# A graph network's first stage: products, turn and counts reordered within each quarter, and the next group's first turn moved into this group's last quarter

## The chip, the core and the metric

The kernel runs on one core of a Trainium2 chip. A core has five engines with a queue of instructions each: PE (TensorE, matrix products), DVE (VectorE), ACT (ScalarE), POOL (GpSimd, which here issues gathers) and SP (SyncE, which issues the other DMAs). They meet only at semaphores: an instruction waits until a counter has reached a value, and another raises it when it is done. The metric is the device time of one launch in microseconds (us); less is better.

## What is computed

The inputs are 12,500 nodes with 32 features, 200,000 edges sorted by target (`dst`) and 16 attributes for each edge. The reference, cut to what matters:

```python
h = relu(layernorm(x))
m = relu(concat([h[src], edge_attr]) @ w1a + b1a) @ w1b + b1b       # one message per edge
agg = segment_sum(m, dst) / max(count(dst), 1)
x = x + relu(concat([h, agg]) @ w2a + b2a) @ w2b + b2b

f = feat0 = relu(layernorm(x))
for _ in range(10):                                                 # propagation
    f = 0.9 * segment_sum((f * out_deg**-0.5)[src], dst) * in_deg**-0.5 + 0.1 * feat0
x = x + f
```

## The kernel before

The program prepares keys and degrees (up to about 185 us), then runs `messages_and_counts` (to about 2825 us), then `nodes_of_runs` (the node layer) and `propagate` (ten steps of dense products with a table of edge counts, from about 3000 us to the end). The change is in `messages_and_counts` alone.

That function does two jobs at once for 98 *groups*. A group g is 16 edges on each of the 128 partitions (2048 edges), and also 32 windows of 4 target nodes. A group has four *quarters* q.

- **Messages.** POOL gathers the source rows of 16 columns of edges, one indirect DMA for each column, into one of seven row buffers, seven groups ahead. PE *turns* a quarter of them (`turn_rows(q)`: two transposes, L1333, into bank `T_BANK`), ACT copies that to SBUF (`keep_turned`, L1262, tile `turn`), PE multiplies it by the weights (`mix(q)`: four float32 products that the profile counts as 8 matmuls, L1351, into `M_BANK`), and ACT applies relu into `run_sums` (`relu_messages`, L1266). DVE adds these along runs of one target (`add_run`, L1184, sixteen in the first half of the next group) and SP stores them.
- **Counts.** DVE makes 0/1 matrices: `part_hot` for a quarter (L1219) and `place_hot` for each of its 8 windows (L1223). PE multiplies them: `count(r)`, r = 0 to 15, four for each quarter, each with two matmuls of L1316 into one of four banks and two of L1322 into a bank of running sums. ACT copies each bank of two counts out (`read_counts(u)`, u = 0 to 7, L1257). I call these copies **read 0 to read 7**; read u needs counts 2u and 2u+1. SP stores them.

On **PE** the order in a group is: turn 0, mix 0, then the sixteen counts, with turn q+1 behind the second count of quarter q and mix q+1 behind its third. `mix(q)` waits until ACT has copied turn q and has applied relu to the products of the quarter before. On odd groups `mix(3)` also turns the keys of the next pair of groups (L1291); on even groups mix 0 waits until DVE has read them (`local_made`). **ACT** follows in the order: copy of turn 0, relu 0, read 0, copy of turn 1, read 1, relu 1, read 2, and so on.

**POOL** (`step`) refills the row buffer of group g in eight pairs of gathers, u = 0 to 7. The first pair waits for turn 3 of group g and for the indices. The others wait for ACT (`count_read`, L1092): pairs 1 and 2 for reads 6 and 7 of group g, and pairs 3 to 7 for reads 0 to 4 of group g+1. On odd groups one gather of keys (L1075) comes before. The last 7 groups have no gathers.

The semaphore `turned` counts the turns; SP (L1133) and POOL (L1082) wait for it by number. PE's and ACT's code runs in a hardware loop of 7 rounds of 14 groups, as DVE's does; POOL's and SP's run 6 rounds and write out the last one.

## Time and profile before

| | |
|---|---|
| median of 3 runs | 7052.78 us (7047.1 to 7060.38) |
| the profiled execution's own time | 7054.22 us |
| its span, first to last instruction | 7052.7 us |
| PE busy in the span | 5638.9 us (80%) |
| DVE busy | 4287.4 us (61%) |
| POOL busy | 1693.6 us (24%) |
| ACT busy | 713.1 us (10%) |

A time of the profiled execution can be compared with the median of the runs directly: they are 1.4 us apart. A share of the whole span is an average over stages that have different limits, so the stage of the change has to be read by itself: it holds nearly all of ACT's and POOL's work and little of PE's. Idle time before an instruction is given with what ended it; "remote" there means that a semaphore rose at a moment at which the records show no instruction ending, and "issue" that nothing it waited for rose just then. A matmul's record starts when the engine takes it; its end is modelled.

### The profile page before, as it was taken

How to read it: one execution, taken by the hardware profiler on the slowest of the kernel's cores; microseconds unless marked ns; L12 is line 12 of the kernel's file. 1: busy time of each engine (PE TensorE's matmuls, PEld its weight loads, DVE VectorE, ACT ScalarE, POOL GpSimd, SP SyncE). 2: the span in 40 equal slices, each digit the busy share in tenths (PEclk: the TensorE clock that was granted, in tenths of full speed). 3: DMA queues.
4: the chain of work that ended last, by engine and by line, in shares of the span. 5: the costliest groups of instructions: out<-in, count | busy, mean ns of one | idle time of the engine just before them, and what ended most of it. 6: DMA issues, size and time to landing. Idle time of an engine off the chain costs nothing. (4 is left out here: it accounts for less than half of the span.)

```text
span 7052.7 us, 211605 instructions
## 1 busy us (share of the span) xinstructions
PE 5638.9 (80%) x85008; PEld 3706.2 (53%) x85008; DVE 4287.4 (61%) x12668; ACT 713.1 (10%) x1695; POOL 1693.6 (24%) x1739
## 2 busy tenths in 40 slices
PE   1455565655555557589999999999999999999998
PEld 1355454544454446446565565656555565656564
DVE  7455555555555557766656666666656666666665
ACT  0122222222222223000000000000000000000000
POOL 5555555555555552500000000000000000000000
PEclk9766666666667667799999999999999999999999
DMA  4322222222222222145555555555555555555554
GB/s 118 76 75 76 75 75 75 75 71 78 73 79 72 75 75 90 37 186 192 200 190 200 190 200 200 190 200 190 200 191 199 191 202 202 187 203 191 199 197 170
DMA packets 442865, 1016.62 MB, mean 144 GB/s; under 512 B 253162, under 2 KB 371914, under 8 KB 387354
## 3 DMA queue, kind: packets, MB, share of 16 engines
q1 hardware_dynamic: 386938, 968.76, 38.8%
q0 software_dynamic: 54944, 33.96, 2.6%
q8 instruction: 714, 11.70, 0.6%
q14 instruction: 269, 2.20, 0.1%
HBM read 838.78 MB, written 176.58 MB: 144 GB/s over the span
## 5 line engine op out<-in xcount | busy, mean ns | idle before, releaser
L1866 PE MATMUL banks_fast<-count_units_fast,feature_parts_fast 128*32 128x512 fp8e3 x70608 | 3826.2, 379 | 31.6 <-DVE count_units_fast L1761 27.0
L1866 PEld LDWEIGHTS banks_fast<-count_units_fast,feature_parts_fast 128*32 128x32 bf16 x70608 | 2154.4, 97 | 1680.2 <-issue 37.4
L1760 DVE TENSOR_SCALAR count_units_fast<-packed_ring_fast 128x512 int32<-128x512 int32 x2949 | 1257.0, 426 | 1427.4 <-PE banks_fast L1866 1396.9
L144 POOL DMA_INDIRECT rows_fast<-row_table,idx_fast x1456 | 1408.6, 967 | 1034.7 <-ACT count_stage_fast L1257 615.7
L1761 DVE TENSOR_SCALAR count_units_fast<-packed_ring_fast 128x512 int32<-128x512 int32 x2949 | 1238.8, 420 | 0.0
L1351 PE MATMUL banks_fast<-w1a_b1a_fast,turn_fast 49*128 49x96 f32 x3136 | 404.4, 399 | 905.1 <-ACT turn_fast L1262 561.4
L1223 DVE TENSOR_SCALAR window_place_hot_fast<-iota_wide_fast,local_keys_fast,target_weight_fast 128x196 bf16<-128x196 f16 x3136 | 939.3, 345 | 0.0
L1351 PEld LDWEIGHTS banks_fast<-w1a_b1a_fast,turn_fast 49*128 49x128 f32 x3136 | 319.6, 281 | 1015.8 <-issue 633.5
L1316 PE MATMUL banks_fast<-window_place_hot_fast,window_src_hot_fast 128*128 128x196 bf16 x3136 | 747.1, 335 | 29.5 <-DVE window_place_hot_fast L1223 25.9
L1322 PE MATMUL banks_fast<-window_place_hot_fast,window_src_hot_fast 128*128 128x196 bf16 x3136 | 728.7, 328 | 6.1 <-issue 6.0
L1219 DVE TENSOR_TENSOR window_src_hot_fast<-iota_by_windows_fast,window_keys_fast 128x1024 bf16<-128x1024 bf16 x392 | 269.6, 688 | 499.1 <-remote 364.1
L1257 ACT CAST count_stage_fast<-banks_fast 128x392 uint16<-128x392 f32 x784 | 383.9, 501 | 1594.8 <-remote 830.2
L1316 PEld LDWEIGHTS banks_fast<-window_place_hot_fast,window_src_hot_fast 128*128 128x128 bf16 x3136 | 418.2, 158 | 133.8 <-issue 78.3
L1184 DVE SCALAR_TENSOR_TENSOR run_sums_fast<-run_sums_fast,same_target 128x96 f32<-128x96 f32 x1485 | 461.5, 311 | 34.6 <-remote 21.6
L1322 PEld LDWEIGHTS banks_fast<-window_place_hot_fast,window_src_hot_fast 128*128 128x128 bf16 x3136 | 467.4, 159 | 5.4 <-issue 5.4
L1744 ACT COPY drained_fast<-banks_fast 128x512 f32<-128x512 f32 x60 | 35.2, 586 | 3839.9 <-PE banks_fast L1866 3839.9
L1198 DVE COPY key_idx_fast<-window_row 64x1 int32 x49 | 7.2, 146 | 473.0 <-ACT run_sums_fast L1266 404.8
L1333 PE MATMUL banks_fast<-identity_fast,rows_fast 128*128 128x128 f32 x784 | 215.0, 366 | 12.1 <-issue 11.8
L1266 ACT ACTIVATE run_sums_fast<-banks_fast 128x384 f32<-128x384 f32 x392 | 193.8, 494 | 156.1 <-PE banks_fast L1351 133.8
L1291 PE MATMUL banks_fast<-identity_fast,raw_keys_fast 128*128 128x64 f32 x200 | 49.6, 394 | 177.2 <-issue 97.2
L1262 ACT COPY turn_fast<-banks_fast 128x256 f32<-128x256 f32 x392 | 150.5, 384 | 231.7 <-remote 174.7
L1424 POOL DMA_INDIRECT feature_parts_fast<-running_sums,run_last_idx_fast x98 | 104.2, 1063 | 150.2 <-DVE run_last_idx_fast L1429 106.5
(282 smaller groups left out, 1646.7 us busy)
## 6 DMA issues: line engine op xcount, KB each, us to landing
packed_ring_fast<-edge_counts SPq DMA_DIRECT2D x422, 1792.0 KB, 7.0
edge_counts<-count_stage_fast SPq DMA_DIRECT2D x100, 784.0 KB
running_sums<-run_sums_fast SPq DMA_DIRECT2D x100, 768.0 KB
rows_fast<-row_table,idx_fast POOLq DMA_INDIRECT x1456
rows_fast<-attrs_padded SPq DMA_DIRECT2D x98, 128.0 KB
attrs_padded<-in_edge_attr SPq DMA_DIRECT2D x1, 12500.0 KB
rows_fast<-row_table,src_ends_fast POOLq DMA_INDIRECT x112
row_table<-h_nodes_fast SPq DMA_DIRECT2D x1, 1568.0 KB, 5.2
```

Of the source, the lines that this page charges most:

```text
L144: pool.indirect_dma_start(out=self.rows[:, r, c, 0:DN], out_offset=None, in_=b.dram.table, in_offset=bass.IndirectOffsetOnAxis(ap=idx[:, c ...
L1184: nc.vector.scalar_tensor_tensor(out=sums[:, s, c, :], in0=before, scalar=same[:, at], in1=sums[:, s, c, :], op0=ALU.mult, op1=ALU.add).th ...
L1219: nc.vector.tensor_tensor(part_hot[:, q % 2, :, :], iota_by_windows[:, :, :], keys[:, s * WG + q * QW:s * WG + (q + 1) * QW].unsqueeze(1). ...
L1223: nc.vector.tensor_scalar(place_hot[:, q % 2, w, :], iota_w[:, :], local[:, at:at + 1], weight[:, at:at + 1], ALU.is_equal, ALU.mult).then ...
L1257: nc.scalar.copy(to, of).then_inc(count_read, 1)
L1316: last = nc.tensor.matmul(b.banks[:, C_BANK[u % 4], side * WC:(side + 1) * WC], part_hot[:, m, :, w], place_hot[:, m, w, :], start=(half = ...
L1322: last = nc.tensor.matmul(b.banks[:, S_BANK, half * WC:(half + 1) * WC], part_hot[:, m, :, w], place_hot[:, m, w, :], start=False, stop=Fa ...
L1333: last = nc.tensor.transpose(b.banks[:, T_BANK, k * P:(k + 1) * P], rows[:, r_rows, c:c + 2, :].rearrange("p c d -> p (c d)"), b.ident[:, :])
L1351: last = nc.tensor.matmul(b.banks[:, M_BANK + k % 2, k // 2 * DH:(k // 2 + 1) * DH], turn[at:at + DI + 1, q % 2, (k // 2) * P:(k // 2 + 1) ...
L1760: nc.vector.tensor_scalar(to[..., 0:P // 8], of, NIBBLES, None, ALU.bitwise_and)
L1761: return nc.vector.tensor_scalar(to[..., P // 8:P // 4], of, 4, NIBBLES, ALU.logical_shift_right, ALU.bitwise_and)
L1866: last = nc.tensor.matmul(b.banks[at:at + DN, SWEEP[m % 2], 0:COLS], parts[:, side, j, k * DN:(k + 1) * DN], of_strip.bitcast(FP8), start= ...
```

## The change

Four edits, all in `messages_and_counts`.

1. **PE's order in a quarter** becomes mix q, turn q+1, then the four counts of quarter q. Before, the turn stood behind the second of these counts and the next mix behind the third.
2. **The turn of the next group's first quarter** is issued in quarter 3 of this group, between mix 3 and count 12, with its waits for that group's rows and attributes (`rows_in`). The very first one is issued ahead of the loop.
3. **ACT's order** follows: relu q, copy of turn q+1, read 2q, read 2q+1. In quarter 3 the copy is that of the next group's turn 0.
4. **The last of the 7 rounds** is written out behind the loop on PE and on ACT, because its last group has no turn to issue for a next group. PE's and ACT's programs are longer by that round.

No instruction of the engines is added or removed otherwise; the thresholds of the semaphores count the same turns and copies as before.

```diff
 # ACT
+            def keep_turned(n, slot):
+                act.wait_ge(turned, n + (SLOTS * Q + 1))
+                nc.scalar.copy(turn[:, slot, :], b.banks[:, T_BANK, 0:2 * P]).then_inc(turn_read, 1)
+            keep_turned(0, 0)
...
-                    keep_turned(0)
                     act.wait_ge(sums_out[s], (k + 1) * 16)
                     act.sem_inc(passed, 1)
-                    relu_messages(0)
-                    act.wait_ge(counts_out[s], (k + 1) * 16)
-                    act.sem_inc(passed, 1)
                     for u in range(READS):
+                        q, at = divmod(u, QW // 4)
+                        if at == 0:
+                            relu_messages(q)
+                        if at == 0 and not (last_loop and t == BATCH - 1 and q == Q - 1):
+                            keep_turned(g * Q + q + 1, (q + 1) % 2)
+                        if u == 0:
+                            act.wait_ge(counts_out[s], (k + 1) * 16)
+                            act.sem_inc(passed, 1)
                         read_counts(u)
-                        q, at = divmod(u, QW // 4)
-                        if q < Q - 1 and at == 0:
-                            keep_turned(q + 1)
-                        if q < Q - 1 and at == 1:
-                            relu_messages(q + 1)
 # PE
-                    turn_rows(0)
-                    mix(0)
                     for r in range(WG // 2):
+                        q, at = divmod(r, QW // 2)
+                        if at == 0:
+                            mix(q)
+                        if at == 0 and q < Q - 1:
+                            turn_rows(r_rows, q + 1)
+                        if at == 0 and q == Q - 1 and not (last_loop and t == BATCH - 1):
+                            rows_in((t + 1) % AHEAD_GROUPS, i * (BATCH // AHEAD_GROUPS) + (t + 1) // AHEAD_GROUPS)
+                            turn_rows((t + 1) % AHEAD_GROUPS, 0)
                         count(r)
-                        q, at = divmod(r, QW // 2)
-                        if q < Q - 1 and at == 1:
-                            turn_rows(q + 1)
-                        if q < Q - 1 and at == 2:
-                            mix(q + 1)
+            with pe.Fori(0, n_loops - 1) as i:
+                one_loop(i, False)
+            one_loop(n_loops - 1, True)
```

What this does to PE's queue, in quarter 0 and at the start of quarter 1. First the kernel before: L1316 and L1322 are a count, L1333 is a turn, L1351 a mix.

```order
L1351 MATMUL banks_fast<-w1a_b1a_fast,turn_fast 128x96 x3
L1310 ISA
L1313 ISA [waits window_hot_fast]
L1316 MATMUL banks_fast<-window_place_hot_fast,window_src_hot_fast 128x196 [waits counts_read_fast]
...
L1333 MATMUL banks_fast<-identity_fast,rows_fast 128x128 x2
L1310 REGISTER_ALU
L1313 REGISTER_ALU [waits window_hot_fast]
L1316 MATMUL banks_fast<-window_place_hot_fast,window_src_hot_fast 128x196 [waits counts_read_fast]
L1316 MATMUL banks_fast<-window_place_hot_fast,window_src_hot_fast 128x196
L1322 MATMUL banks_fast<-window_place_hot_fast,window_src_hot_fast 128x196 x2
L1339 REGISTER_ALU
L1351 MATMUL banks_fast<-w1a_b1a_fast,turn_fast 128x96 [waits mix_read_fast,pairs_read_fast]
```

Then the changed kernel, where L1336 and L1342 are a count, L1317 is a turn and L1360 a mix.

```order
L1360 MATMUL banks_fast<-w1a_b1a_fast,turn_fast 128x96 x3
L1317 MATMUL banks_fast<-identity_fast,rows_fast 128x128 x2
L1330 ISA
L1333 ISA [waits window_hot_fast]
L1336 MATMUL banks_fast<-window_place_hot_fast,window_src_hot_fast 128x196 [waits counts_read_fast]
...
L1330 REGISTER_ALU
L1336 MATMUL banks_fast<-window_place_hot_fast,window_src_hot_fast 128x196 [waits window_hot_fast]
L1336 MATMUL banks_fast<-window_place_hot_fast,window_src_hot_fast 128x196
L1342 MATMUL banks_fast<-window_place_hot_fast,window_src_hot_fast 128x196 x2
L1348 REGISTER_ALU
L1360 MATMUL banks_fast<-w1a_b1a_fast,turn_fast 128x96 [waits mix_read_fast,pairs_read_fast]
```

The fourth count, on which read 1 rests, now stands ahead of mix 1, and four counts stand between turn 1 and mix 1 instead of one.

The end of a group on PE, before: the last count, then the next group's turn with its wait for rows, and mix 0 right behind it.

```order
L1322 MATMUL banks_fast<-window_place_hot_fast,window_src_hot_fast 128x196 x2
L1333 MATMUL banks_fast<-identity_fast,rows_fast 128x128 [waits attrs_in2_fast,gathered2_fast]
L1333 MATMUL banks_fast<-identity_fast,rows_fast 128x128
L1339 ISA
L1341 REGISTER_ALU [waits pairs_read_fast]
```

After, in quarter 3 of an odd group: the keys' turn, mix 3, the next group's turn, then counts.

```order
L1356 ISA [waits mix_read_fast,pairs_read_fast]
L1296 MATMUL banks_fast<-identity_fast,raw_keys_fast 128x64 [waits keys_in1_fast]
L1296 MATMUL banks_fast<-identity_fast,raw_keys_fast 128x64
L1360 MATMUL banks_fast<-w1a_b1a_fast,turn_fast 128x96 x4
L1317 MATMUL banks_fast<-identity_fast,rows_fast 128x128 [waits attrs_in2_fast,gathered2_fast]
L1317 MATMUL banks_fast<-identity_fast,rows_fast 128x128
L1330 REGISTER_ALU
L1333 REGISTER_ALU [waits window_hot_fast]
L1336 MATMUL banks_fast<-window_place_hot_fast,window_src_hot_fast 128x196 [waits counts_read_fast]
```

The next group's turn moved ahead of the four counts of quarter 3.

## Rows read from the trace of the kernel before

**Rows 1.** Stretches by stage: us, busy us of each engine, granted clock, DMA share.

```profile
600.00:1000.00 400.00, 233.37 (x1532) 200.16 (x1532) 223.56 (x857) 98.53 (x237) 231.37 (x240) 0.63 0.28 76
2705.00:2810.00 105.00, 82.28 (x636) 68.14 (x636) 90.50 (x352) 42.41 (x101) 13.70 (x14) 0.76 0.27 94
```

**Rows 2.** Groups by line, 600 to 2600 us: busy, mean ns, idle before.

```profile
L144 POOL DMA_INDIRECT rows_fast<-row_table,idx_fast x1170 | 1130.5, 966 | 824.4 <-ACT count_stage_fast L1257 503.0 <-issue 318.6 <-remote 1.8
L1075 POOL DMA_INDIRECT raw_keys_fast<-edge_keys,key_idx_fast x36 | 32.6, 905 | 11.8 <-issue 11.8
L1245 ACT ACTIVATE first_act_fast<-zeros_fast 128x1 f32<-128x1 f32 x6 | 1.2, 203 | 9.3 <-issue 9.3
```

**Rows 3.** Timeline of POOL: start, us, instruction, idle before it and its end.

```profile
1503.95 0.94 POOL L144 DMA_INDIRECT rows_fast<-row_table,idx_fast  x1 [3.77 <-ACT count_stage_fast L1257]
...
1510.32 1.02 POOL L144 DMA_INDIRECT rows_fast<-row_table,idx_fast  x1 [0.30 <-issue]
1514.20 0.94 POOL L144 DMA_INDIRECT rows_fast<-row_table,idx_fast  x1 [2.86 <-ACT count_stage_fast L1257]
...
1516.69 1.36 POOL L144 DMA_INDIRECT rows_fast<-row_table,idx_fast  x1 [0.30 <-issue]
...
1527.07 0.94 POOL L144 DMA_INDIRECT rows_fast<-row_table,idx_fast  x1 [0.30 <-issue]
1531.50 0.94 POOL L144 DMA_INDIRECT rows_fast<-row_table,idx_fast  x1 [3.48 <-ACT count_stage_fast L1257]
...
1541.72 0.94 POOL L144 DMA_INDIRECT rows_fast<-row_table,idx_fast  x1 [2.65 <-ACT count_stage_fast L1257]
...
1558.28 0.94 POOL L144 DMA_INDIRECT rows_fast<-row_table,idx_fast  x1 [4.38 <-ACT count_stage_fast L1257]
```

**Rows 4.** Timeline of ACT, same columns.

```profile
1506.87 0.51 ACT L1257 CAST count_stage_fast<-banks_fast 128x392 uint16<-128x392 f32 x1 [1.18 <-PE banks_fast L1316]
1509.72 0.37 ACT L1262 COPY turn_fast<-banks_fast 128x256 f32<-128x256 f32 x1 [2.34 <-remote]
...
1519.25 0.37 ACT L1262 COPY turn_fast<-banks_fast 128x256 f32<-128x256 f32 x1 [0.89 <-remote]
1529.39 0.49 ACT L1257 CAST count_stage_fast<-banks_fast 128x392 uint16<-128x392 f32 x1 [9.77 <-remote]
...
1530.23 0.87 ACT L1257 CAST count_stage_fast<-banks_fast 128x392 uint16<-128x392 f32 x2
...
1534.68 0.49 ACT L1257 CAST count_stage_fast<-banks_fast 128x392 uint16<-128x392 f32 x1 [1.33 <-PE banks_fast L1316]
```

**Rows 5.** Timeline of PE, same columns.

```profile
1506.39 0.63 PE L1333 MATMUL banks_fast<-identity_fast,rows_fast 128*128 128x128 f32 x2
...
1516.80 0.33 PE L1316 MATMUL banks_fast<-window_place_hot_fast,window_src_hot_fast 128*128 128x196 bf16 x2
...
1521.55 0.55 PE L1316 MATMUL banks_fast<-window_place_hot_fast,window_src_hot_fast 128*128 128x196 bf16 x2
...
1524.83 0.63 PE L1333 MATMUL banks_fast<-identity_fast,rows_fast 128*128 128x128 f32 x2
1531.62 1.18 PE L1351 MATMUL banks_fast<-w1a_b1a_fast,turn_fast 49*128 49x96 f32 x8 [6.15 <-DVE window_base_fast L1212]
...
1534.01 0.55 PE L1316 MATMUL banks_fast<-window_place_hot_fast,window_src_hot_fast 128*128 128x196 bf16 x2
```

**Rows 6.** Timeline of DVE: eight `place_hot` with `add_run` between (first, last), eight without.

```profile
1507.15 0.33 DVE L1223 TENSOR_SCALAR window_place_hot_fast<-iota_wide_fast,local_keys_fast,target_weight_fast 128x196 bf16<-128x196 f16 x1
...
1510.44 0.32 DVE L1223 TENSOR_SCALAR window_place_hot_fast<-iota_wide_fast,local_keys_fast,target_weight_fast 128x196 bf16<-128x196 f16 x1
...
1517.15 2.18 DVE L1223 TENSOR_SCALAR window_place_hot_fast<-iota_wide_fast,local_keys_fast,target_weight_fast 128x196 bf16<-128x196 f16 x8
```

**Rows 7.** Timeline of ACT: copy of turn 0 in groups 93 and 97.

```profile
2746.19 0.38 ACT L1262 COPY turn_fast<-banks_fast 128x256 f32<-128x256 f32 x1
...
2809.53 0.38 ACT L1262 COPY turn_fast<-banks_fast 128x256 f32<-128x256 f32 x1
```

More of the change, by code:

```diff
@@ L1241, in _, with one_loop @@
             act.sem_inc(count_read, SLOTS * READS)
-            with act.Fori(0, n_loops) as i:
+            def keep_turned(n, slot):
+                act.wait_ge(turned, n + (SLOTS * Q + 1))
+                nc.scalar.copy(turn[:, slot, :], b.banks[:, T_BANK, 0:2 * P]).then_inc(turn_read, 1)
+            keep_turned(0, 0)
+            def one_loop(i, last_loop):
                 nc.scalar.activation(first_act[:, :], b.zeros[:, 0:1], ACT.Relu).then_inc(first_done, 1)
@@ L1257, in read_counts @@
                         nc.scalar.copy(to, of).then_inc(count_read, 1)
-                    def keep_turned(q):
-                        act.wait_ge(turned, SLOTS * Q + g * Q + (q + 1))
-                        nc.scalar.copy(turn[:, q % 2, :], b.banks[:, T_BANK, 0:2 * P]).then_inc(turn_read, 1)
                     def relu_messages(q):
@@ L1301, in _, with rows_in, turn_rows, one_loop @@
             pe.sem_inc(turned, SLOTS * Q)
-            with pe.Fori(0, n_loops) as i:
+            def rows_in(r_rows, turns):
+                pe.wait_ge(gathered[r_rows], (turns + 1) * (G * 16))
+                pe.wait_ge(attrs_in[r_rows], (turns + 1) * 16)
+            def turn_rows(r_rows, q):
+                for k in range(QC // 2):
+                    c = q * QC + 2 * k
+                    last = nc.tensor.transpose(b.banks[:, T_BANK, k * P:(k + 1) * P],
+                                               rows[:, r_rows, c:c + 2, :].rearrange("p c d -> p (c d)"), b.ident[:, :])
+                last.then_inc(turned, 1)
+            rows_in(0, 0)
+            turn_rows(0, 0)
+            def one_loop(i, last_loop):
                 for t in range(BATCH):
-                    g, pair, s, r_rows, turns = (i * BATCH + t, i * PAIRS_A_LOOP + t // SLOTS, t % SLOTS, t % AHEAD_GROUPS,
-                                                 i * (BATCH // AHEAD_GROUPS) + t // AHEAD_GROUPS)
+                    g, pair, s, r_rows = i * BATCH + t, i * PAIRS_A_LOOP + t // SLOTS, t % SLOTS, t % AHEAD_GROUPS
                     def count(r):
@@ L1324, in count @@
                         last.then_inc(hot_used, 1)
-                    pe.wait_ge(gathered[r_rows], (turns + 1) * (G * 16))
-                    pe.wait_ge(attrs_in[r_rows], (turns + 1) * 16)
-                    def turn_rows(q):
-                        for k in range(QC // 2):
-                            c = q * QC + 2 * k
-                            last = nc.tensor.transpose(b.banks[:, T_BANK, k * P:(k + 1) * P],
-                                                       rows[:, r_rows, c:c + 2, :].rearrange("p c d -> p (c d)"), b.ident[:, :])
-                        last.then_inc(turned, 1)
                     def mix(q):
```

3 lines of the change are left out of this document (added).

## Prediction

> **What bounds the kernel now.** The first view is that of the busy time by stage. The change touches only the stage from about 185 to 2825 us. While gathers run, no engine is busy for even 60% of it: PE 233 of 400 us, POOL 231, DVE 224, ACT 99 [rows 1]. The last seven groups have no gathers, and they go by faster. Groups 93 to 97 take (2809.53 - 2746.19) / 4 = 15.8 us each [rows 7]. With gathers a group takes 27.35 us: 1170 gathers, 16 for each group, are 73.1 groups in 2000 us [rows 2]. So PE, ACT and DVE can do a group in 15.8 us, and gathering costs 11.5 us more.
>
> The second view is the groups by line. POOL's 27.35 us are 16 gathers of 0.966 us, their pauses of about 0.3, half a gather of keys (together 20.5), and 503.0 / 73.1 = 6.9 us of waiting for ACT's reads (L1257) [rows 2]. POOL's queue is thus the pacemaker: 20.5 us of its own and 6.9 us of stops.
>
> The third view is POOL's timeline: it runs in two **runs** for each group. Six gathers (1503.95 to 1511.34, pairs 1 to 3), a stop of 2.86 us, eleven (1514.20 to 1528.01, pairs 4 to 7, the next pair 0, keys), a stop of 3.48, six again, 2.65, ten, 4.38 [rows 3]. The four stops of two groups are 13.4 us.
>
> The fourth view, ACT's timeline beside PE's, says why POOL stops. PE's second count after 1505 ends by its record near 1506.3 and ACT reads it at 1506.87; the turn behind it ends at 1507.02, and ACT's copy starts at 1509.72, 2.7 us late [rows 4, 5]. Worse at the end of the group: all PE's work, the next turn too, is recorded by 1525.46, and ACT's read 5 starts only at 1529.39 with a wait ended by "remote" [rows 4, 5]. During a run of gathers PE's ends become known late, and 1.4 us after the run's last gather ended (1528.01) they come all at once: reads 6 and 7 follow at 1530.23 [rows 3, 4]. From these rows I take four properties, as estimates:
> - the first 2 to 3 us of a run are prompt: the run from 1531.50 has PE's count ended at 1534.56 and read at 1534.68 [rows 3 to 5];
> - after that PE's ends come one by one. Between 1506.87 and 1509.72 four matmuls ended (two of L1322, two of the turn): 0.71 us each. Between 1519.25 and 1529.39 it was 18 (a count of 4, keys 4, products 8, half a count): 0.56 us each;
> - they come free about 1.4 us after the run; then relu, read and POOL's start take until 2.9 to 4.4 us after it;
> - what counts is how many matmuls lie between a run's prompt phase and the read that POOL needs next.
>
> **The change, part by part.** No instruction is added to the loop. So nothing of PE's 15.8 us or POOL's 20.5 us changes; the change can only move stops.
>
> *Fourth count ahead of mix 1.* Before, read 1 (POOL's pair 4) lies behind mix 1, and mix 1 waits for ACT's copy of turn 1, which is late. That is the first stop. After, call F the moment at which the ends come free at the end of a group. ACT does relu 3, the copy of turn 0, read 6 (0.4 to 0.5 us each): F+1.3; POOL starts at F+2.1. PE starts mix 0 at F+0.9, since the copy is no longer behind reads 5 to 7 and the turn; before, it was 2.2 us after read 5 began (1531.62 against 1529.39) [rows 4, 5]. Then mix (1.2), turn (0.5), and four counts at DVE's pace with run sums, 0.47 us for a window ((1510.44 - 1507.15) / 7, 3.8 us for eight) [rows 6]: count 3 is done at about F+5. The run is prompt until F+4.1 to F+5.1, so read 1 comes between F+5 and F+8 (four ends at 0.71). POOL wants it after six gathers, at F+2.1+7.6 = F+9.7. The first stop goes and the run becomes eight gathers.
>
> *What is late next.* Read 2 (pair 5) now lies behind mix 1 and turn 2: from about F+4.7 the ends in front are count 3 (4), mix (8), turn (2), and count 4 with half of 5 (6), 20 in all, 11 to 14 us at 0.56 to 0.71. POOL is through its eight at F+12.1. So it stops there: free 1.5 us later, relu 1, copy, read 2 and the wake add 2.1. That is 3.1 to 3.7 us, in place of 2.9.
>
> *The second run.* Call F' that next release. Mix 2 starts at F'+0.9, turn 3 and counts 8 and 9 are done by F'+3.8 (counts at the half clock are (1524.83 - 1521.55) / 5 = 0.66 us apart [rows 5], and DVE needs only 2.2 us for eight windows without run sums [rows 6]), still prompt, so read 4 is in time and the run is pairs 5, 6, 7 and the next pair 0: eight gathers, nine with keys, until F'+12.1 to F'+13.4. Read 6 decides what then: in front of it are mix 3 (8), keys (4, on odd groups), turn (2), counts 12 and half 13 (6), so 16 to 20 ends, or 9 to 14 us from F'+5: F'+14 to F'+19 by the slow rate, F'+13 by the fast one on an even group. That is about even. If it comes late, there is a second stop as now, 3.8 to 4.0 us. If in time, the run goes on into the next group's pairs 1 to 4 and becomes 12 or 13 long.
>
> *The sum for a group.* Two stops remain in each group: 3.4 + 3.8 = 7.2 against 6.9, so +0.3 at worst, 0 at best. One of four is saved: three stops in two groups, 3.1 + 3.8 + 3.7 = 10.6 against 13.4, so -1.4 to -1.6 for a group. I take a pattern that is half of each, -0.7, because the deciding read lies on the edge. It holds for the 91 groups with gathers: -64 us. Both ends are kept for the range: -145 and +25.
>
> *Turn 0 moved into quarter 3.* Its wait for the next rows is free, since these were gathered six groups ago. In the 7 groups without gathers the round trip turn, copy, mix is hidden; DVE is busy for 90.5 of 105 us there [rows 1], so that it has at most 2 us of 15.8 to give back in each; I take 0.3, since its short waits for its own results stay: -2 us, between -14 and 0.
>
> *The last round written out.* ACT idles 9.3 / 6 = 1.55 us at a round's start for "issue" [rows 2]; one such start goes: -2 us, between -2 and +3 if the longer code is late itself.
>
> SP waits for the same turns by number, and its loads are five groups ahead: 0.
>
> The sum is 7054.2 - 64 - 2 - 2 = 6986; less the 1.4 us by which the profiled execution lies above the median, **6985 us**.
>
> A rule that speaks against the change: gathers of 0.94 us are the common ones, but one (1516.69) took 1.36 us beside DVE's unbroken eight `place_hot` (1517.15) [rows 3, 6]; the mean is 0.966 [rows 2], so all such delay is 16 x 0.026 = 0.4 us for a group now. The Trainium skill, "SBUF — State Buffer", on who interferes with whom, says that a VectorE operation in a two-port mode locks GpSimd out and that descriptors of its DMAs are then not written. By that rule, with a gather held up in each of the four quarters, a group would cost 4 x 0.42 - 0.4 = 1.3 us more and the sum would be near 7100; by the row it stays at 0.4, and the sum as it is.
>
> **The rivals.**
>
> *A stop saved in every pair of groups* (runs of 8, 12, 13 throughout). For it: 0.56 us for an end is the longer measurement of the two. Against: on odd groups 20 ends do not fit in 8 us. Time: 7054 - 145 = 6910. A faster PE would bring it: the granted clock is 0.63 here, so most of the time is at 1.2 GHz, where a pair of L1316 takes 0.55 us (1521.55), against 0.33 at 2.4 GHz (1516.80) [rows 1, 5]. The Trainium skill, "TensorE: Matmul & The Clock Gate", section on HAM oscillation, advises keeping TensorE's work together, since idle stretches bring the half clock back. Mix, turn and four counts now stand in one piece; by that rule the clock rises, counts 8 to 11 end up to 1.3 us earlier (half of four times 0.66), read 6 is in time, and the sum is this rival's.
>
> *Only exchanged stops.* Every read 6 is late: two stops for each group, 6.9 to 7.2. For it: the ends in front of read 6 are as many as before. Time: 7054 to 7080.
>
> *A third stop, slower.* Its place is read 4 (pair 7). Behind mix 2, turn 3, counts 8 and 9, it is done at F'+3.8, and the run begins at F'+2.1. If the prompt phase is shorter than 1.7 us, up to 16 ends stand in front at 0.56 or more, and POOL, done with pairs 5 and 6 at F'+7.1, stops again. A third stop is 2.7 us (after a short run), less 1.2 because it starts the prompt phase again for read 6: +1.5 for a group, 7054 + 137 = 7190 if always, 7120 if in every second group. For it: at 1507.02 a turn 3.1 us into a run was already late. Against: 3.18 us was prompt in another [rows 3 to 5].
>
> *The order changes nothing* because POOL's stops depend on something else than ends: then also a shorter round trip is worth nothing, 7052.
>
> **How the numbers follow.** The half and half pattern 0.50 (6950 to 7035), the saving everywhere 0.15, exchanged or unchanged 0.19, the third stop 0.16. The least difference from no change that a measurement of this kernel tells is about 0.2%, 14 us. Faster: 0.48 of the first, 0.15, and 0.05 of the third: 0.68. Same: 0.02 and 0.08: 0.10. Slower: 0.06 and 0.16: 0.22. The range leaves out the far end of the third stop and a full saving with a higher clock: 6900 to 7095.
>
> **What would show it.** In the profile after: the stage up to `nodes_of_runs` ends about 70 us earlier and the rest is as long as before. POOL's waits for ACT's reads fall from 6.9 to about 6.2 us for a group, its own 20.5 us stay. Its runs are 8 to 13 long, none of six. Read 1 starts within 8 us of mix 0's release and no stop precedes pair 4. The stops that are left are before pair 5 and, in half of the groups, before pair 1. I am wrong if runs of six remain, if a stop before pair 7 shows, if gathers are longer than 0.97 us on the mean, or if the granted clock rises well over 0.68 and takes the time with it.

## The result and the profile after

The changed kernel takes **7032.48 us** (median of 20 runs, 7018.96 to 7052.25) and the kernel before 7058.13 us beside it (20 runs, 7042.45 to 7070.84): ratio **0.9968**, 95% interval 0.9960 to 0.9976. It is faster, by 0.32% where 0.96% was forecast (6985 against 7052.78 us). The profiled execution took 7024.77 us (span 7022.8), before 7054.22 (7052.7): 29.4 us less.

The difference has two parts of opposite sign. First the stage of the change, in the views that answer to [rows 1, 2]: two stretches of the changed kernel (us, busy us of each engine, granted clock, DMA share),

```profile
600.00:1000.00 400.00, 231.03 (x1585) 190.71 (x1586) 223.09 (x848) 103.16 (x244) 236.71 (x244) 0.70 0.28 75
2700.00:2755.00 55.00, 47.61 (x396) 37.07 (x394) 53.97 (x213) 26.25 (x60) 0.00 (x0) 0.91 0.28 103
```

The clock has risen from 0.63 to 0.70, and without gathers DVE is busy for 54 of 55 us. The groups by line from 600 to 2600 us:

```profile
L144 POOL DMA_INDIRECT rows_fast<-row_table,idx_fast x1194 | 1157.9, 970 | 799.1 <-ACT count_stage_fast L1263 460.8 <-issue 335.7 <-PE banks_fast L1317 2.4
```

1194 gathers are 74.6 groups, so a group takes 26.80 us (27.35 before), of which POOL waits for ACT's reads 460.8 / 74.6 = 6.18 us (503.0 / 73.1 = 6.88 before). That is by the releaser the profile names. All of POOL's pauses over 1 us together, some of them put down to "issue", are 6.36 us for a group, before 6.93; there are 146 of them in these 2000 us, before 169. The stage runs from the first mix at 184.4 to the last read at 2770.6: 2586.2 us, before 2637.7. That is **51.5 us less**. POOL's timeline, which answers to [rows 3]:

```profile
1510.88 0.94 POOL L144 DMA_INDIRECT rows_fast<-row_table,idx_fast  x1 [3.38 <-ACT count_stage_fast L1263]
...
1519.83 0.94 POOL L144 DMA_INDIRECT rows_fast<-row_table,idx_fast  x1 [0.30 <-issue]
1523.80 0.94 POOL L144 DMA_INDIRECT rows_fast<-row_table,idx_fast  x1 [3.03 <-ACT count_stage_fast L1263]
...
1540.28 0.94 POOL L144 DMA_INDIRECT rows_fast<-row_table,idx_fast  x1 [3.72 <-ACT count_stage_fast L1263]
...
1553.20 0.94 POOL L144 DMA_INDIRECT rows_fast<-row_table,idx_fast  x1 [3.08 <-ACT count_stage_fast L1263]
1554.45 0.95 POOL L144 DMA_INDIRECT rows_fast<-row_table,idx_fast  x1 [0.30 <-issue]
1555.70 0.90 POOL L1075 DMA_INDIRECT raw_keys_fast<-edge_keys,key_idx_fast  x1 [0.30 <-issue]
```

From 1510.88 eight gathers, then ten, then eight. The gather of keys at 1555.70 closes a group, so the stop at 1553.20 is before pair 7 of that group. In the 70 groups from 14 on, with the gather of keys counted and a pause of over 1 us ending a run, there are 66 runs of eight, 49 of nine to twelve and 5 of six; before, 73 of six. The stops' places are:

| | stops for a group | before pair 1 | 3 | 4 | 5 | 7 | other |
|---|---|---|---|---|---|---|---|
| before | 2.31 | 56 | 19 | 51 | 0 | 9 | 27 |
| after | 1.97 | 27 | 30 | 9 | 20 | 33 | 19 |

Second, `propagate`, which the diff doesn't touch. Its products, all 70608, with their first and last start, after and then before:

```profile
L1879 PE MATMUL banks_fast<-count_units_fast,feature_parts_fast x70608: 376/379/634, 2982.8 to 6992.2; 128*32 128x512 fp8e3 x200
```

```profile
L1866 PE MATMUL banks_fast<-count_units_fast,feature_parts_fast x70608: 376/379/634, 3036.8 to 7020.3; 128*32 128x512 fp8e3 x200
```

That is 4009.4 us after and 3983.5 before: **25.9 us more**. The products themselves take the same 379 ns. PE's waits for "issue" in this stretch are 29.6 us, before 11.6. The largest of them come at one place, once in two steps. Here is PE's timeline at one of four such places (3786, 4588, 5390 and 6192 us):

```profile
4585.19 1.16 PE L1847 MATMUL banks_fast<-unit_identity_fast,drained_fast 128*128 128x128 f32 x8
4586.43 1.48 PE L1879 MATMUL banks_fast<-count_units_fast,feature_parts_fast 128*32 128x512 fp8e3 x24
4592.47 12.88 PE L1879 MATMUL banks_fast<-count_units_fast,feature_parts_fast 128*32 128x512 fp8e3 x204 [4.56 <-issue]
```

`propagate` is a hardware loop of five passes of two steps, and this is where it jumps back: four jumps, four stalls of 3.9 to 4.9 us (1.0 to 1.3 before), during which PE waits for no semaphore that the profile shows. Smaller stalls of 1.0 to 1.7 us stand near the middle of the steps in both kernels. -51.5 and +25.9 are -25.6; the remaining 4 us lie ahead of the groups (1.8), between the stages (0.7) and behind the propagation (1.8).

### The profile page after: what moved, and what is told of

Read it like the earlier page. It is cut to its first block and busy times, and to the rows that moved or that the text cites. A ratio compares the mean times of both kernels' runs of the same rounds, so it can differ in the third digit from the quotient of the medians.

```text
span 7022.8 us, 211083 instructions
## 1 busy us (share of the span) xinstructions
PE 5636.0 (80%) x85008; PEld 3556.5 (51%) x85008; DVE 4289.5 (61%) x12668; ACT 725.0 (10%) x1695; POOL 1697.1 (24%) x1739
## 3 DMA queue, kind: packets, MB, share of 16 engines
q8 instruction: 715, 11.71, 0.6%
## 5 line engine op out<-in xcount | busy, mean ns | idle before, releaser
L1879 PEld LDWEIGHTS banks_fast<-count_units_fast,feature_parts_fast 128*32 128x32 bf16 x70608 | 2047.9, 97 | 1805.8 <-issue 59.9
L1360 PE MATMUL banks_fast<-w1a_b1a_fast,turn_fast 49*128 49x96 f32 x3136 | 399.4, 395 | 643.2 <-ACT turn_fast L1246 472.9
L1336 PE MATMUL banks_fast<-window_place_hot_fast,window_src_hot_fast 128*128 128x196 bf16 x3136 | 712.9, 317 | 154.6 <-issue 106.7
L1342 PE MATMUL banks_fast<-window_place_hot_fast,window_src_hot_fast 128*128 128x196 bf16 x3136 | 699.4, 312 | 114.7 <-issue 110.9
L1360 PEld LDWEIGHTS banks_fast<-w1a_b1a_fast,turn_fast 49*128 49x128 f32 x3136 | 316.1, 278 | 747.7 <-ACT turn_fast L1246 458.1
L1336 PEld LDWEIGHTS banks_fast<-window_place_hot_fast,window_src_hot_fast 128*128 128x128 bf16 x3136 | 433.7, 157 | 242.3 <-issue 156.1
L1342 PEld LDWEIGHTS banks_fast<-window_place_hot_fast,window_src_hot_fast 128*128 128x128 bf16 x3136 | 446.6, 156 | 120.7 <-issue 120.7
L1317 PE MATMUL banks_fast<-identity_fast,rows_fast 128*128 128x128 f32 x784 | 229.5, 387 | 0.0
```

The costliest lines, as they stand in the source:

```text
L1317: last = nc.tensor.transpose(b.banks[:, T_BANK, k * P:(k + 1) * P], rows[:, r_rows, c:c + 2, :].rearrange("p c d -> p (c d)"), b.ident[:, :])
L1336: last = nc.tensor.matmul(b.banks[:, C_BANK[u % 4], side * WC:(side + 1) * WC], part_hot[:, m, :, w], place_hot[:, m, w, :], start=(half = ...
L1342: last = nc.tensor.matmul(b.banks[:, S_BANK, half * WC:(half + 1) * WC], part_hot[:, m, :, w], place_hot[:, m, w, :], start=False, stop=Fa ...
L1360: last = nc.tensor.matmul(b.banks[:, M_BANK + k % 2, k // 2 * DH:(k // 2 + 1) * DH], turn[at:at + DI + 1, q % 2, (k // 2) * P:(k // 2 + 1) ...
L1879: last = nc.tensor.matmul(b.banks[at:at + DN, SWEEP[m % 2], 0:COLS], parts[:, side, j, k * DN:(k + 1) * DN], of_strip.bitcast(FP8), start= ...
```

## Experiments

Chips differed in a way that decides how these are read. On some the kernel before took 7017 to 7058 us, on others 6385 to 6387 us, and there POOL hardly ever stopped. I call them *stopping* and *non-stopping* chips. Every batch of runs had one chip at one time, so that the chip and the moment can't be told apart. Each ratio is against the kernel before on the same chip. "Padding" is small products of zeros, two instructions each, on PE.

### Which part of the change does what

**e1, e4: the last round written out, nothing else** (e4 on PE alone), on a non-stopping chip.

```diff
-            with pe.Fori(0, n_loops) as i:
+            def one_loop(i):
...
+            with pe.Fori(0, n_loops - 1) as i:
+                one_loop(i)
+            one_loop(n_loops - 1)
```

> The kernel before, with only the last of the 7 rounds written out on PE and ACT (order as before). Theory A, the longer programs move the code of the propagation loop and PE then waits for its code there: the groups keep their 27.3 us, the stage of the groups is as long as before within 3 us, and the ten propagation steps are about 25 us longer in all (every second one by 6 to 7 us), so the time is 7080 us, 1.0035 of before. Rival B, the steps are longer for another reason (earlier start, other clock): propagation as before, time 7056 us, 0.998 to 1.001.

> The kernel before with the last round written out on PE alone. Theory A with PE's code as the place of the wait: 7080 us, as with both engines. Rival: ACT's longer code is the cause, then 7056 us.

Measured: e1 6406.64 us, ratio 1.0035 (1.0021 to 1.0048); e4 6411.81, 1.0043 (1.0030 to 1.0057). e1's propagation:

```profile
L1874 PE MATMUL banks_fast<-count_units_fast,feature_parts_fast x70608: 376/379/634, 2369.2 to 6378.2; 128*32 128x512 fp8e3 x200
```

4009.0 us. With PE's round alone (e4) it is 4006.2 us. So writing out the round costs by itself what the changed kernel lost there, and PE's part of it is enough.

**e2, e9: order and turn ahead, all seven rounds in the loop** (the first group of each round turns its own first quarter), on a non-stopping chip (e2) and on a stopping one (e9). PE's part, against the changed kernel:

```diff
+                    if t == 0:
+                        rows_in(0, i * (BATCH // AHEAD_GROUPS))
+                        turn_rows(0, 0)
...
-                        if at == 0 and q == Q - 1 and not (last_loop and t == BATCH - 1):
+                        if at == 0 and q == Q - 1 and t < BATCH - 1:
```

> The changed order and the turn ahead, but in 7 rounds of the loop as before: the last group of a round issues no turn for the next, and the first group of a round issues its own turn 0 at its start (7 of 98 groups). Theory A: the groups gain nearly as in the changed kernel (stage shorter by 45 to 51 us), propagation as in the kernel before; 7010 us, 0.993 of before, 22 us less than the changed kernel. Rival B: propagation is again about 25 us longer; 7035 us.

> The changed order and the turn ahead, but PE's and ACT's seven rounds all in the loop (the first group of each round turns its own first quarter), beside a kernel before that takes about 7057 us. My theory: the group stage ends about 50 us earlier than before, as in the changed kernel, and the propagation keeps its length of 3984 us with steps of 398 us, so that the time is 7008 us, ratio 0.993 (0.992 to 0.995), faster than the changed kernel by 25 us. Rival (the written-out round also helps the groups, or the chip decides): about 7032, ratio 0.9965. If the kernel before takes about 6385 us on this chip: ratio 0.996, as it was once.

Measured: e2 6360.81 us, 0.9962 (0.9949 to 0.9976). e9 **6970.09 us, 0.9932** (0.9917 to 0.9946), on a chip where the kernel before took 7017.30. e9's propagation is 3983.2 us and its stage is 2556.9 us long, with POOL waiting 432.4 / 75.5 = 5.7 us for reads in a group:

```profile
L144 POOL DMA_INDIRECT rows_fast<-row_table,idx_fast x1208 | 1176.6, 974 | 777.0 <-ACT count_stage_fast L1262 432.4 <-issue 339.0 <-PE banks_fast L1317 5.0
```

**e5, e12: the order in a quarter alone**, each group turning its own first quarter at its start, on a non-stopping chip (e5) and a stopping one (e12). **e6: the turn ahead alone**, behind mix 3 in the old order, on a stopping one. The diff is e5 and e12 against e9, whose condition for the first quarter's turn at the group's start goes too; e6 puts such a turn behind mix 3 in the kernel before.

```diff
-                        if at == 0 and q == Q - 1 and t < BATCH - 1:
-                            rows_in((t + 1) % AHEAD_GROUPS, ...)
-                            turn_rows((t + 1) % AHEAD_GROUPS, 0)
```

> Only the order within the quarters: mix, turn, four counts; the turn of quarter 0 stands at the start of its own group as before, no round is written out. If the order carries the gain (read 1 ahead of mix 1, runs of six gathers become eight): 0.4 to 0.5 us for a group, 7015 us. If the turn ahead carries it (mix 0 starts sooner after the release): 7050 us.

> Only the order within the quarters of the change (mix, turn, counts), the turn of a group's first quarter at its own start, all rounds in the loop. My theory, beside a kernel before of about 7057 us: the order alone brings runs of eight in place of runs of six, and most of the gain of 0.4 us for a group; the propagation keeps 3984 us: 7020, ratio 0.995 (0.993 to 0.997). Rival (the turn ahead is what brings it; without it mix 0 waits for a late copy at a group's start): runs of six stay and the ratio is 1.000. If the kernel before takes about 6385 us here: 1.000.

> Only the turn ahead: the old order within the quarters; the next group's turn 0 stands behind mix 3 (except at the end of a round), its copy behind relu 3; no round written out. Where POOL never stops: the order alone gave nothing there and both together 25 us, so if the turn ahead is the cause the stage is 20 to 25 us shorter, 0.9965 of before; if only both together give it, 1.000. Where POOL stops: read 1 stays behind mix 1, runs of six stay; 0.1 to 0.3 us for a group from the sooner mix 0, 0.997 to 0.999.

Measured: e5 6387.60 us, 1.0002 (0.9993 to 1.0011); e12 6988.41, **0.9955** (0.9940 to 0.9971); e6 7044.07, **0.9985** (0.9975 to 0.9995). On stopping chips the order gives 28.9 us, the turn ahead 12.7, and both together 47.2 (e9): they add up, with 5.6 us over, which the intervals cover. On a non-stopping chip the order is worth nothing, and the 26.8 us between e5 and e2, on one chip, are what the turn ahead adds to it there. e6 keeps the runs of six (58 of them); e12 has 30 of six and 44 of eight. So the order by itself removes somewhat more than half of the runs of six.

### What POOL's stops are

**e8: the kernel of e9, but POOL doesn't wait for ACT's reads** (the wait for turn 3 stays), on a stopping chip.

```diff
-                    if u:
-                        pool.wait_ge(count_read, (SLOTS + g + 1) * READS - READS // Q + u)
-                        pool.sem_inc(taken, 1)
```

> As the experiment without the written-out round, and POOL no longer waits for ACT's reads between its pairs of gathers: all 16 follow in one run after turn 3 of their group. Where POOL never stops: no change against that experiment, 0.996 of before. Where it stops: if the stops come from these waits alone, a group falls towards POOL's own 20.5 us (0.93 to 0.95 of before); if from PE's ends being late while gathers run, turn 3 of the next group is late as well, one stop of 4 to 6 us for each group remains and the time is within 2% of before.

Measured: 7442.70 us, 1.0551 (1.0535 to 1.0566), where e9 has 0.9932: 6% more than the kernel it was made from. Both of my expectations failed, and it is the most telling run. POOL now gathers all 16 in one piece and then waits for turn 3 (the profile writes "issue"):

```profile
1512.43 0.94 POOL L144 DMA_INDIRECT rows_fast<-row_table,idx_fast  x1 [0.30 <-issue]
1524.99 0.90 POOL L1075 DMA_INDIRECT raw_keys_fast<-edge_keys,key_idx_fast  x1 [11.61 <-issue]
...
1545.14 0.94 POOL L144 DMA_INDIRECT rows_fast<-row_table,idx_fast  x1 [0.30 <-issue]
1556.89 0.94 POOL L144 DMA_INDIRECT rows_fast<-row_table,idx_fast  x1 [10.81 <-issue]
```

ACT's timeline beside the first two of these rows:

```profile
1505.56 0.49 ACT L1259 CAST count_stage_fast<-banks_fast 128x392 uint16<-128x392 f32 x1 [8.42 <-remote]
1516.64 0.49 ACT L1264 ACTIVATE run_sums_fast<-banks_fast 128x384 f32<-128x384 f32 x1 [10.60 <-remote]
1517.03 0.37 ACT L1243 COPY turn_fast<-banks_fast 128x256 f32<-128x256 f32 x1
1517.28 0.90 ACT L1259 CAST count_stage_fast<-banks_fast 128x392 uint16<-128x392 f32 x2
```

While POOL gathers, ACT gets one release from PE in 19 us; the greater part of the group is then done in the 11 us of the stop and the 2 us behind it. A group takes 31.6 us. So a stop isn't only lost time: it is where PE's work is finished. Runs of 8 to 10 with stops of 3 to 4 us beat one of 16 with a stop of 11.

**e7: the first of each pair of gathers alone, in all groups after the first seven** (half of the rows are not gathered), on a stopping chip.

```diff
-                    ahead.gather(pool, b, r, idx[:, r, :], range(u * G // READS, (u + 1) * G // READS))
+                    ahead.gather(pool, b, r, idx[:, r, :], range(u * G // READS, u * G // READS + 1))
```

> The kernel before with 8 instead of 16 gathers for each group behind the first seven groups (the rows of the other columns are old ones; messages are wrong, the work on the other engines is the same). POOL's own part falls from 20.5 to 10.5 us. Theory of the late ends: they are late only while gathers run, so a group falls to between 16 and 18 us, DVE's pace, on either kind of chip. If something else than POOL's gathers held the groups at 27 or 21 us, they stay above 20 us.

Measured: 6129.92 us, 0.8683 (0.8667 to 0.8699). A group takes 17.2 us in place of 27.3, near the 15.8 without gathers [rows 7]: eight gathers fewer are worth 10.1 us, 1.26 us each, about a gather with its pause. The match is no proof of POOL's pace: DVE is busy for 344 of 400 us there (224 before), so the group lies close to what the other engines need, and the 6.5 us for which POOL still waits in a group can't be told from waiting for them.

**The same start on both kinds of chip.** In the first groups POOL gathers without a stop on both. PE's timeline in e9 (stopping), group 1:

```profile
216.82 0.32 PE L1340 MATMUL banks_fast<-window_place_hot_fast,window_src_hot_fast 128*128 128x196 bf16 x1 [2.48 <-issue]
218.93 0.32 PE L1340 MATMUL banks_fast<-window_place_hot_fast,window_src_hot_fast 128*128 128x196 bf16 x1 [1.78 <-issue]
221.72 0.32 PE L1334 MATMUL banks_fast<-window_place_hot_fast,window_src_hot_fast 128*128 128x196 bf16 x1 [2.47 <-issue]
```

and in g2 (below, non-stopping):

```profile
210.53 0.39 PE L1336 MATMUL banks_fast<-window_place_hot_fast,window_src_hot_fast 128*128 128x196 bf16 x2
210.75 0.33 PE L1342 MATMUL banks_fast<-window_place_hot_fast,window_src_hot_fast 128*128 128x196 bf16 x2
211.10 0.39 PE L1336 MATMUL banks_fast<-window_place_hot_fast,window_src_hot_fast 128*128 128x196 bf16 x2
```

One product in 2.1 to 2.8 us against two in 0.2 to 0.4. From its first mix to the next group's the first group takes 58 us in e9 and 16 in g2. Both chips issue gathers of 0.95 us every 1.25 us there.

### Why an unchanged loop grew

The rival was length: more code, more delay. The theory: what counts is where the loop's code starts. The page's row on the instruction queue (packets, MB, share) speaks for looking at stretches of 256 instructions:

```profile
q8 instruction: 715, 11.71, 0.6%
```

A packet is 11.71 MB / 715 = 16.4 KB. The Trainium skill, "Runtime: NRT & Kernel Launch", section "Instruction fetch mechanics", says that instructions come in blocks of 16 KiB, 256 of them, and that a taken branch out of the blocks at hand has to fetch its target first. The trace agrees on the size of a block. The same section calls the cost of crossing a block mostly hidden and says nothing of the target's place in it; the runs below do.

**e10** is e9 with 190 instructions of padding ahead of the group stage, **e11** the changed kernel with 66; both on a stopping chip. e10's expectation took the written-out round for 2494 instructions, 190 more than nine times 256. **f1 to f4 and g1** are e9 with padding right ahead of `propagate`, **g2** is the changed kernel with it; all on non-stopping chips.

```diff
+            for _ in range(95):
+                nc.tensor.matmul(b.banks[:, SWEEP[0], 0:8], b.zeros16[:, :], b.zeros16[:, 0:8], start=True, stop=True)
             pe.wait_ge(stacked, STRIPS + 1)
```

> The kernel of e9 with 95 small matmuls of zeros added on PE ahead of the group stage (190 instructions more in the program's count, which is what the written-out round adds, 2494, less nine times 256), where PE waits for its first keys anyway. Theory of position (a stretch of 256 instructions is what counts, and the loop of the propagation starts at another place in one): stalls of 3.8 to 4.9 us on PE once for every two steps of the propagation, which is 4009 us long. Rival of length (it is the 2494 instructions more that count, or the round's code behind the loop): the propagation stays at 3984 us, no such stall. Groups as in e9.

> The changed kernel with 33 small matmuls of zeros added on PE ahead of the group stage (66 instructions in the program's count, so that the addition of the written-out round and these is 2560, ten times 256). Theory of position: no stall once in two steps, the propagation is 3984 us long, and the time is some 25 us below the changed kernel, about 7008, ratio 0.993. Rival of length: stalls stay, 4009 us, 7032, ratio 0.9965.

> The kernel of e9 with 95 small matmuls of zeros (190 instructions in the program's count) added on PE right ahead of the propagation, where no gather runs, in place of e10's, which stood ahead of the group stage and cost some 12 us there. Theory of position: the propagation's loop starts where it started in e10, so it is 3970 us long in place of 3983 (the two stalls of 0.8 to 1.7 us for each two steps go), and the groups are as in e9: some 10 to 13 us below e9, ratio 0.991 to 0.992 beside a before of 7017 to 7057 us (0.994 beside one of 6385). Rival (e10's shorter propagation came from its start elsewhere in time, or from chance): 3983 us, 0.993.

> As f1 with 32 matmuls (64 instructions). Only the length of the propagation and its PE stalls are looked at: by position it lies somewhere between 3970 and 4009 us, and another value than 3983.3 (within 1 us) shows position at work with 64 instructions already; by the rival of length it is 3983.

> As f1 with 159 matmuls (318 instructions, 128 more than f1). If what counts is the place within a stretch of 128 instructions or less, the propagation is as long as f1's, 3970 us; if the stretch is longer, it is another value between 3970 and 4009. By the rival of length: 3983.

> As f1 with 223 matmuls (446 instructions, 256 more than f1). If what counts is the place within a stretch of 256 instructions, the propagation is as long as f1's, 3970 us; if the stretch is longer, another value up to 4009. By the rival of length (more code, more delay): longer than f3.

> The kernel of f1 once more. On a chip on which the kernel before takes some 7017 to 7057 us: propagation 3970 us, groups as in e9 (2557 to 2575 us), ratio 0.991 (0.990 to 0.993), faster than the changed kernel by some 40 us. On one where it takes 6385 us: 0.994 again.

> The changed kernel with 63 small matmuls of zeros (126 instructions in the program's count) ahead of the propagation. Its propagation of 4009 to 4010 us is that of f2 (64 on top of the code without the written-out round: 4009.1). If the round put the loop's start where f2 has it, 126 more put it where f1 has it (190): 3970 us, and the time is that of g1 within 10 us. Rival (the written-out round costs the propagation something of its own): more than 3980 us.

Measured (the length is from the first start of such a product to the last):

| kernel | instructions added | `propagate`, us | time, us | ratio |
|---|---|---|---|---|
| e9 | 0 | 3983.2 | 6970.09 | 0.9932 (0.9917 to 0.9946) |
| f2 | 64 | 4009.1 | 6385.67, one run | |
| f1, g1 | 190 | 3969.1, 3970.3 | 6349.51, 6348.28 | 0.9942 (0.9928 to 0.9955), 0.9939 (0.9925 to 0.9952) |
| e10 | 190, earlier | 3970.1 | 6973.34, two runs | 0.9933 (0.9911 to 0.9956) |
| f3 | 318 | 4016.1 | 6396.45, one run | |
| f4 | 446 | 3970.0 | 6348.10, one run | |
| after | the round | 4009.4 | 7032.48 | 0.9968 (0.9960 to 0.9976) |
| e11 | the round + 66 | 3976.9 | 6961.44 | 0.9914 (0.9900 to 0.9929) |
| g2 | the round + 126 | 3970.5 | 6346.87 | 0.9940 (0.9926 to 0.9953) |

The rows of f2, f3 and f4 behind the table, in this order:

```profile
L1879 PE MATMUL banks_fast<-count_units_fast,feature_parts_fast x70608: 376/379/634, 2343.4 to 6352.5; 128*32 128x512 fp8e3 x200
```

```profile
L1879 PE MATMUL banks_fast<-count_units_fast,feature_parts_fast x70608: 376/379/634, 2347.1 to 6363.2; 128*32 128x512 fp8e3 x200
```

```profile
L1879 PE MATMUL banks_fast<-count_units_fast,feature_parts_fast x70608: 376/379/634, 2345.5 to 6315.5; 128*32 128x512 fp8e3 x200
```

And the jump back in f2, with its stall, then PE at the same passage in g2, without one:

```profile
3946.01 1.91 PE L1879 MATMUL banks_fast<-count_units_fast,feature_parts_fast 128*32 128x512 fp8e3 x31 [0.28 <-issue]
3951.46 13.81 PE L1879 MATMUL banks_fast<-count_units_fast,feature_parts_fast 128*32 128x512 fp8e3 x200 [3.54 <-issue]
```

```profile
3933.27 1.16 PE L1847 MATMUL banks_fast<-unit_identity_fast,drained_fast 128*128 128x128 f32 x8
3934.36 25.87 PE L1879 MATMUL banks_fast<-count_units_fast,feature_parts_fast 128*32 128x512 fp8e3 x468
```

Length is refuted: f4 has the most padding and is among the shortest, and e11 and g2 are the changed kernel with yet more code and lose its stalls. That the place counts is shown: 190 and 318, 128 apart, differ by 47 us. For a period of 256 speak 190 and 446, which are 256 apart and agree within 0.9 us, and 64 and 318, which are 254 apart, are both long and differ by 7 us; it is one pair at the exact distance. g2 said beforehand that the changed kernel sits where f2 does and needs 126 more to be at f1's place, and it came out at 3970.5. The kernel before is not at the best place either: 13 us lie there.

Two expectations of the theory missed. In e10 the propagation was to be 4009 us long, like the changed kernel's, and was 3970.1; in e11 it was to be 3984 and was 3976.9. Both rested on the length of the round, and that count doesn't hold: 2494 takes two instructions for a product, while the trace has 106 matmul records in a group, 8 for a mix of four products, and so 2968 matmuls and weight loads in a round, waits not counted. That the changed kernel sits where f2 does was read from its 4009 us, not counted.

What PE waits for at a stall is in the traces. The rows of the instruction queue from the first product to the last, in the changed kernel and in g2:

```profile
q8 instruction: 609, 9.98, 1.0%
```

```profile
q8 instruction: 605, 9.91, 1.0%
```

Packets of 16.4 KB come every 6.6 us on the mean. In all six traces in which this stretch is 4006 to 4016 us long (after, a1, e1, e4, f2, f3) there are 609, in the other fourteen, of 3969 to 3984 us, 604 or 605: four jumps back, and four packets more. And each stall ends soon after such a packet. In the stretch shown above a packet lands at 4590.98 us and PE goes on at 4592.47. PE's 138 gaps of over 0.9 us in this stretch, in all 20 traces, end 1.2 to 1.8 us after the landing of a packet, where one in ten would by chance; f1, f4, g1, g2 and e10 have no such gap. So the stalls are waits for code. Why a block comes too late near the middle of a step as well isn't shown.

In e10 the earlier padding gave those 13 us back, since its products of zeros ran beside POOL's gathers and the stage ended 12.1 us later than e9's (2754.1 against 2742.0):

```profile
161.82 1.79 PE L1305 MATMUL banks_fast<-zeros_fast 128*128 128x8 bf16 x54
164.04 0.30 PE L1305 MATMUL banks_fast<-zeros_fast 128*128 128x8 bf16 x6 [0.43 <-issue]
...
175.54 0.17 PE L1305 MATMUL banks_fast<-zeros_fast 128*128 128x8 bf16 x1 [1.23 <-issue]
177.64 0.17 PE L1305 MATMUL banks_fast<-zeros_fast 128*128 128x8 bf16 x1 [1.94 <-issue]
```

These products wait for no semaphore and raise none. 54 of them go at once and then one in 1.3 to 2 us.

**The changed kernel again (a1)**, beside e6, e7 and e8 on their chip.

> The changed kernel itself, beside the kernel before on the same chip. Where POOL never stops (as on the chip of the first four experiments, where the kernel before took 6385 us): the sum of the two parts measured there, 25 us less in the groups and 25 us more in the propagation, 1.000 of before. Where POOL stops twice in a group (kernel before near 7055 us): 0.997 as in the first comparison.

Measured: 7041.72 us, 0.9975 (0.9965 to 0.9984), stage 2594.8 us, propagation 4010.0: the same two parts again.

**The best version** is the order and the turn ahead with the loop at its best place: 0.994 on non-stopping chips (f1, g1, g2; the changed kernel's group stage is not faster there than e2's). On stopping ones only its parts ran: e11, 7 us off the best place, has 0.9914 (6961.44 us).

## Why the prediction was wrong, point by point

- **What bounds the stage: right for the chips of this comparison, not for all.** POOL's queue sets the pace and stops for ACT's reads. On the other kind of chip there are hardly any stops and a group takes 20.8 to 21.2 us. The prediction had put POOL's own part at 20.5 [rows 2].
- **The first stop goes: right. Where the next ones come: wrong.** 73 runs of six became 5, and a stop before pair 4 stands in 9 groups of 70 instead of 51. But the forecast had the stops that are left before pair 5 in every group and before pair 1 in half of them, and named a stop before pair 7 as a sign of being wrong. They stand before pair 7 in 33 groups of 70, pair 3 in 30, pair 1 in 27 and pair 5 in 20. So the half and half pattern didn't come about. That the waits for reads fell by 6.88 - 6.18 = 0.70 us for a group, as forecast, is in part luck: there are 1.97 stops for a group in place of 2.31, of 3.27 us in place of 3.00.
- **The term of the groups, -64: too large by a quarter.** 0.55 us for a group over 91 groups is 50 us. POOL's own part stayed, as forecast: its gathers and pauses of up to 1 us are 20.43 us for a group, before 20.35. What was too large is the saving in stops, 0.57 us by all pauses over 1 us (6.93 to 6.36) where 0.70 was forecast. With the two small terms the prediction had -66 or -68 for the stage and it was -51.5.
- **The turn ahead, -2: too small.** Alone it gave 12.7 us (e6). In the groups without gathers, where the 2 us were to come from, a group takes 14.9 us in place of 15.8 (groups 93 to 97), 0.9 less where 0.3 was taken. The rest comes with gathers running; that mix 0 no longer stands behind the turn's round trip is the likely reason, not shown by itself. I had put it down as part of the order's pattern; e12 shows 28.9 us for the order without it. Together they are the 47 of e9, against 66 forecast.
- **The last round written out, "-2 us, between -2 and +3": the step that failed.** It cost 25.9 us, in `propagate`. I looked for its cost only where the written-out code runs. It lay in what stands behind it in PE's program: e1 and e4 show the cost alone, f1 to f4 and g2 that it is the place of a loop's code, and the instruction queue's packets that PE waits for code there. "The rest is as long as before" was the line of the list that told it.
- **The sum.** Of the profiled execution -68 us were forecast and -29.4 measured. The stage's -51.5 instead of -66 is 15 us of the miss, the written-out round 28 (+25.9 in place of -2), and the 4 us elsewhere go the other way. Without the written-out round the ratio is 0.9932 (e9, on another chip), and the forecast ratio was 0.990.
- **The rivals.** A saving in every pair of groups (1.5 stops for a group) and a third stop added to two are out by the count of 1.97. Exchanged stops, two in every group, have the count right, but not the places, and the stops are 6.4 us for a group where that rival has 6.9 to 7.2. The third stop's place, pair 7, is where a stop is most often found now. That POOL's stops depend on something other than how many matmuls lie in front has some truth: e8 shows that the work isn't delayed by a fixed time but hardly goes on at all while gathers run. By the rule of the Trainium skill, "SBUF — State Buffer", on who interferes with whom, the prediction had 1.3 us more for a group, about 0.08 us for a gather. They went from 0.966 to 0.970 us, so the trace doesn't bear it out here.
- **The clock**: 0.70 where it had been 0.63 from 600 to 1000 us. That is a little over the 0.68 named as a warning. I had tied the full saving to it, and the full saving didn't come.

## What to carry to other kernels

Read the stages that a change doesn't touch as carefully as the one it does: whatever lengthens an engine's program moves every loop behind it. If a hot loop's stall sits at its jump back, shift its code by some padding where the engine is idle and look again before judging the change. And before a stop is removed, ask what gets done in it: here the engine that was waited for made its progress in the stops, and with none of the waits for reads the kernel was 5.5% slower than before. And where a forecast names the places at which an engine will stop, count them afterwards: the size of a saving can come out about right for another pattern.

## What the runs showed that I had not expected

- Chips of one type differ by 10% on this kernel (6385 against 7017 to 7058 us), nearly all of it in the stage with gathers. On the slower kind PE hardly advances while POOL issues gathers, even for products without any semaphore (e10); on the other two products pass in 0.2 to 0.4 us beside them (g2). The gathers are as long on both (0.96 to 0.98 us on the mean). What it is in the chip stays open.
- A loop over two steps of 398 us pays 0 to 5.2 us at its jump back and up to 2.2 us near the middle of a step, by the place of its code: 3969 to 4016 us in all, 1.2%. Which place within the 256 is good was found by trial (0, 62, 64 and 190, and between them the changed kernel with 66 more).
